# Scores before P times V in the first seven batches, inverse row sums spread by ScalarE, last block scaled by ScalarE and stored by the sync queue

## The chip, the cores and the metric

The kernel runs on one core of a Trainium2 chip, in fp32 (large matmuls as three fp32r products of high and low halves). The metric is the device time of one execution in microseconds (us): 685.59 us before, the median of 3 runs (684.93 to 685.87).

## The reference

One post-norm decoder layer on x of shape (8, 256, 512): softmax attention with 16 heads of 32, a decayed recurrence over a context, and a gated feed-forward net whose weights are cubic splines of control points. Cut to what matters:

```python
def heads(y): return y.reshape(B, T, H, dh).transpose(0, 2, 1, 3)
q, k, v = heads(x @ Wq.T), heads(x @ Wk.T), heads(x @ Wv.T)      # then each times Wdown (32 x 32)
scores = einsum('bhqr,bhkr->bhqk', q_r, k_r) / sqrt(32)
y_r = einsum('bhqk,bhkr->bhqr', softmax(scores), v_r)            # then Wup, then Wo
x = layernorm(x + attention)
r_t = decay * r_(t-1) + ctx_t * ctx_t                            # per feature, a scan over 256 tokens
x = layernorm(x + x * r)
x = layernorm(x + (silu(x @ gate.T) * (x @ up.T)) @ down.T)      # gate, up, down: splines, 2048 wide
```

## The kernel before, in words

It is written without a planner: every engine has its own instruction list, in the order of the code, and waits on semaphores. That order is written out by hand, for each engine in a function of its own: `pe_batch`, `act_batch`, `dve_batch`, `pool_batch`, `sp_batch` for a batch of attention, `..._step` for the feed-forward net. PE stands for TensorE, ACT for ScalarE, DVE for VectorE, POOL for GpSimd, SP for the sync queue.

**Attention.** Eight batches `b`, each in four blocks `m` of four heads; block (b,m) below. For one block, TensorE computes the scores S (L478: 16 matmuls, four 32-row tiles at a time, into PSUM banks 0 to 3). VectorE takes the negated row maxima (`dve_max`, L821, one reduction per bank). ScalarE writes exp(S - max) to `probs` and row sums to `rsum` (`act_exp`, L665, eight activations). TensorE transposes `probs` back into banks 0 to 3 (`pe_t`, L490, 16 transposes; it waits for the exp of each head). ScalarE copies head 0 (`act_heads`, L677, signal `pta`) and VectorE heads 1 to 3 (`dve_heads`, L835, signal `ptv`) to `probsT`. VectorE takes the reciprocal of `rsum` into `rinv` and spreads it over 32 columns a head into `rwide` (`dve_inverse`, L827 and L830). TensorE transposes that (`pe_r`, L498) and ScalarE copies it to `Rb` (L680, signal `ra`). TensorE computes P times V (`pe_pv`, L512, four 32-column tiles at a time, 16 matmuls) once `pta`, `ptv` and `ra` are there. VectorE multiplies with `Rb` into `y` (`dve_y`, L785), ScalarE rounds it to `yT` (`act_yh`, L673) and GpSimd takes the low half (`pool_yl`, L921).

Between S and the transposes TensorE runs projections of this or the next batch: `pe_q`, `pe_k` in m = 0 to 2 (m = 0 has the output projection `pe_o` of the batch before instead), `pe_v0`, `pe_v1` in m = 3. The results leave PSUM by ScalarE (`act_qkh`, L653; `act_v`, L659). `pe_extra` puts in one spline tile (b = 1 to 3, L402, copied by VectorE as `spc`, L773) or one weight job (b from 4, L1096, merged by VectorE as `ws`, L1117) before P times V; `pe_q` of m = 3, and `pe_q(nb, 1)`, run in block m = 1 and 2, reuse its bank and wait for `spc` or `ws`. In block m = 2 the four scans of the recurrence (`dve_scan`, L896) stand on VectorE behind `dve_heads`. `dve_size` (L806) stands in m = 3. GpSimd squares the context (L917), rounds x (L909, L911), applies norms (L957, L1002), multiplies (L965) and adds up splines (L936, L940). Batch 7 (`proj` false) has no projections for a next batch.

**Feed-forward.** Four blocks of 512 tokens, eight groups of hidden units in each (`pe_step`: L303 to L305). After the last block each of its four tiles `t` of 128 tokens is finished by `dve_add` (L1408), `dve_out_stats` (L1412), an aggregation (L1594), variance plus eps and power -0.5 on GpSimd (L1638, L1640), `dve_out` (L1426: subtract mean, times inverse deviation) and a store of 256 KB that GpSimd issues (`pool_out`, L1482); on GpSimd all four stores stand behind the four powers.

## Time and profile before

| | us |
|---|---|
| median of 3 runs | 685.59 |
| the profiled execution's own time | 685.51 |
| its span, first to last instruction | 683.7 |
| 0 to 20, loads and first projections | 20 |
| 20 to 340, attention; TensorE busy 313.8 | 320 |
| 340 to 380, end of attention; TensorE busy 35.0 | 40 |
| 380 to 669, feed-forward; TensorE busy 285.2 | 289 |
| 669 to 683.7, last norm and stores | 14.7 |

The profile is of one execution. A row of a timeline is one instruction, or several alike in a row. The busy time of TensorE is modelled and counts a matmul longer than the distance to the next one, so small waits of TensorE are read from the starts of its instructions.

### The profile page before, as it was taken

How to read it: one execution, taken by the hardware profiler on the slowest of the kernel's cores; microseconds unless marked ns; L12 is line 12 of the kernel's file. 1: busy time of each engine (PE TensorE's matmuls, PEld its weight loads, DVE VectorE, ACT ScalarE, POOL GpSimd, SP SyncE). 2: the span in 40 equal slices, each digit the busy share in tenths (PEclk: the TensorE clock that was granted, in tenths of full speed). 3: DMA queues.
4: the chain of work that ended last, by engine and by line, in shares of the span. 5: the costliest groups of instructions: out<-in, count | busy, mean ns of one | idle time of the engine just before them, and what ended most of it. 6: DMA issues, size and time to landing. Idle time of an engine off the chain costs nothing.

```text
span 683.7 us, 12025 instructions
## 1 busy us (share of the span) xinstructions
PE 656.8 (96%) x4312; PEld 533.8 (78%) x4312; DVE 449.5 (66%) x826; ACT 347.7 (51%) x1002; POOL 294.3 (43%) x351
## 2 busy tenths in 40 slices
PE   9999999999999999999988799999999999999993
PEld 9597887878888788788865577888888888888883
DVE  3567687698686877878778688666544555354434
ACT  5566546637466565656667556552334233333230
POOL 1764486886638767594674836100100001000103
PEclk9999999999999999999999999999999999999997
DMA  9621020030220311121112672741193317340301
GB/s 329 221 80 62 1 87 7 2 125 1 94 62 2 133 52 32 63 72 41 40 65 47 159 173 72 210 105 40 35 239 78 81 32 198 72 101 0 124 1 61
DMA packets 22010, 58.06 MB, mean 85 GB/s; under 512 B 4032, under 2 KB 7232, under 8 KB 21056
## 3 DMA queue, kind: packets, MB, share of 16 engines
q1 hardware_dynamic: 16720, 44.45, 22.5%
q0 software_dynamic: 4944, 12.32, 5.9%
q8 instruction: 35, 0.57, 0.3%
q10 hardware_dynamic: 288, 0.52, 0.2%
q14 instruction: 23, 0.19, 0.1%
HBM read 32.11 MB, written 8.39 MB: 59 GB/s over the span
## 4 chain that ended last, share of the span: by engine, by line
PE 78%; DVE 12%; ACT 6%; issue 2%; POOL 1%; DVEq 0%; POOLq 0%; ACTq 0%
PE bank L303 19%; PE bank L305 18%; PE bank L304 18%; PE bank L490 6%; ACT probs L665 5%; PE bank L478 4%; DVE recurrence_T L896 4%; PE bank L512 4%; DVE minus_max L821 3%; PE bank L1191 2%; PE bank L1096 2%; DVE probsT L835 2%; PE bank L529 1%; PE bank L316 1%; PE bank L498 1%
## 5 line engine op out<-in xcount | busy, mean ns | idle before, releaser
L665 ACT ACTIVATE probs<-bank,minus_max 128x256 f32<-128x256 f32 x256 | 117.3, 486 | 23.8 <-DVE minus_max L821 23.8
L303 PE MATMUL bank<-down,hidden_hi_lo 128*128 128x512 f32 x256 | 100.7, 393 | 1.5 <-DVE hidden_hi_lo L1402 1.5
L305 PE MATMUL bank<-down,hidden_hi_lo 128*128 128x512 f32 x256 | 100.5, 392 | 0.0
L304 PE MATMUL bank<-down,hidden_hi_lo 128*128 128x512 f32 x256 | 100.0, 391 | 0.0
L821 DVE TENSOR_REDUCE minus_max<-bank 128x2 f32<-128x512 f32 x128 | 79.3, 681 | 16.3 <-PE bank L478 16.3
L1398 DVE TENSOR_TENSOR hidden<-bank,silu 128x512 f32<-128x512 f32 x64 | 44.1, 689 | 60.9 <-PE bank L305 58.9
L1356 ACT ACTIVATE silu<-bank 128x512 f32<-128x512 f32 x64 | 38.3, 598 | 82.2 <-PE bank L305 81.3
L1402 DVE TENSOR_TENSOR hidden_hi_lo<-hidden,hidden_hi_lo 128x512 fp32r<-128x512 f32 x64 | 45.5, 711 | 40.9 <-ACT hidden_hi_lo L1369 40.8
L490 PE MATMUL bank<-ident,probs 128*128 128x128 f32 x512 | 65.5, 275 | 6.2 <-ACT probs L665 5.9
L1476 POOL TENSOR_TENSOR ffn_var_eps<-ffn_mean_var,constants 128x4 f32<-128x4 f32 x3 | 0.6, 196 | 156.5 <-DVE ffn_mean_var L1418 156.5
L490 PEld LDWEIGHTS bank<-ident,probs 128*128 128x128 f32 x512 | 56.6, 141 | 14.2 <-ACT probs L665 12.0
L1369 ACT CAST hidden_hi_lo<-hidden 128x512 fp32r<-128x512 f32 x64 | 39.8, 622 | 52.3 <-DVE hidden L1398 52.3
L835 DVE COPY probsT<-bank 128x512 f32<-128x512 f32 x96 | 60.1, 680 | 4.8 <-PE bank L490 4.7
L303 PEld LDWEIGHTS bank<-down,hidden_hi_lo 128*128 128x128 f32 x256 | 48.1, 188 | 11.5 <-DVE hidden_hi_lo L1402 1.9
L305 PEld LDWEIGHTS bank<-down,hidden_hi_lo 128*128 128x128 f32 x256 | 48.0, 188 | 10.3
L665 ACT ACTIVATION_READ_ACCUMULATOR probs<-bank,minus_max 128x1 f32 x256 | 55.9, 219 | 0.0
L304 PEld LDWEIGHTS bank<-down,hidden_hi_lo 128*128 128x128 f32 x256 | 48.1, 188 | 9.7
L303 PE MATMUL bank<-xT_hi_lo,wq_hi 128*128 128x256 f32 x128 | 38.7, 303 | 1.1 <-DVE spline_coef_T_down L773 0.4
L303 PE MATMUL bank<-xT_hi_lo,wk_hi 128*128 128x256 f32 x128 | 38.9, 304 | 0.0
L512 PE MATMUL bank<-probsT,V 128*32 128x256 f32 x512 | 36.8, 385 | 0.4 <-ACT inverse_by_query L680 0.4
L478 PE MATMUL bank<-k_heads,q_heads 32*128 32x256 f32 x512 | 36.7, 400 | 0.0
L305 PE MATMUL bank<-xT_hi_lo,wq_lo 128*128 128x256 f32 x128 | 36.1, 282 | 0.0
(170 smaller groups left out, 1610.8 us busy)
## 6 DMA issues: line engine op xcount, KB each, us to landing
features_by_group<-features_by_cell SPq DMA_DIRECT2D x128, 128.0 KB, 2.4
ctx_squared_T<-in_ctxT SPq DMA_DIRECT2D x8, 512.0 KB, 3.3
xres<-in_x SPq DMA_DIRECT2D x8, 512.0 KB, 4.6
x_in<-x SPq DMA_DIRECT2D x16, 256.0 KB, 3.1
x_residual<-x POOLq DMA_DIRECT2D x4, 1024.0 KB, 8.1
out_x<-x_residual POOLq DMA_DIRECT2D x16, 256.0 KB, 2.8
xin_T<-in_xT SPq DMA_DIRECT2D x7, 512.0 KB, 3.9
x<-x_rows SPq DMA_DIRECT2D x7, 512.0 KB, 4.1
```

Source lines behind the costliest of these rows:

```text
L303: nc.tensor.matmul(out, wh, xh, start=first, stop=False)
L304: nc.tensor.matmul(out, wh, xl, start=False, stop=False)
L305: return nc.tensor.matmul(out, wl, xh, start=False, stop=last)
L478: last = nc.tensor.matmul(S[g][:, t * T:(t + 1) * T], qk[0][at, m, t * P:(t + 1) * P], qk[1][at, m, :], start=True, stop=True)
L490: last = nc.tensor.transpose(S[g][:, kt * T + t * P:kt * T + (t + 1) * P], probs[:, g, t, kt * P:(kt + 1) * P], ident[:])
L512: last = nc.tensor.matmul(MI[g * DH:(g + 1) * DH, 0:T], V[:, kt, h * DH:(h + 1) * DH], probsT[:, g, kt, :], start=kt == 0, stop=kt == TT - 1)
L665: inc(nc.scalar.activation(probs[:, g, t, :], S[g][:, t * T:(t + 1) * T], ACT.Exp, bias=nmax[:, g, t:t + 1], accum_out=rsum[:, t, g:g + 1] ...
L821: inc(nc.vector.tensor_reduce(nmax[:, g, :], S[g][:].rearrange("p (t k) -> p t k", t=TT), AX.X, ALU.max, negate=True), "max")
L835: inc(nc.vector.tensor_copy(probsT[:, g, :, :], S[g][:].rearrange("p (k t) -> p k t", k=2)), "ptv")
L1369: inc(nc.scalar.copy(hid[:, g % 2, 0, j, :], hm[:]), "hh")
L1398: inc(nc.vector.tensor_tensor(hm[:], U[:], sg[:], ALU.mult), "hm")
L1402: inc(nc.vector.tensor_tensor(hid[:, g % 2, 1, j, :], hm[:], hid[:, g % 2, 0, j, :].bitcast(F32), ALU.subtract), "hl")
```

## The change

In batches 0 to 6 the scores of block m+1 are issued ahead of P times V of block m, for m = 0 to 2; from block 3 to the next batch the order stays. In batch 0 the last fold matmul stands between the two. VectorE likewise takes the maxima of block m+1 ahead of `dve_y` of block m, and ScalarE does `act_yh` of block m-1 inside `act_exp` of block m, ahead of the fourth head's exps. The four scans of a batch move from behind `dve_heads(b, 2)` to ahead of `dve_inverse(b, 2)`. In all eight batches the spread copy to `rwide` moves from VectorE to ScalarE, where it is the first thing in `act_heads`. In batch 0 the last low half of Wo is taken inside the maxima of block 1. In the last feed-forward block GpSimd computes one more tiny product a tile (minus mean times inverse deviation), ScalarE applies scale and bias in one activation instead of VectorE's `dve_out`, and the sync queue issues the four stores, each behind its tile.

```diff
 def pe_batch(pe, b):
-        if b == 0:
-            pe_fold_o(pe, 3)
-        pe_pv(pe, b, 0)
-        pe_s(pe, b, 1)
+        if proj:
+            pe_s(pe, b, 1)
+            if b == 0:
+                pe_fold_o(pe, 3)
+            pe_pv(pe, b, 0)
+        else:
+            pe_pv(pe, b, 0)
+            pe_s(pe, b, 1)
...
 def act_exp(act, b, m):
         for g in range(HG):
+            if m and g == HG - 1 and b < B - 1:
+                act_yh(act, b, m - 1)
...
+    def act_wide(act, b, m):
+        act.wait_ge(s["rinv"], 4 * b + m + 1)
+        wait(act, "r", 4 * b + m)
+        src = rinv[:].rearrange("p t (g o) -> p t g o", o=1).to_broadcast([P, TT, HG, DH])
+        inc(nc.scalar.copy(rwide[:].rearrange("p t (g o) -> p t g o", g=HG), src), "rwide")
     def act_heads(act, b, m):
+        act_wide(act, b, m)
...
 def dve_max(dve, b, m):
         for g in range(HG):
+            if b == 0 and m == 1 and g == 2:
+                dve_weight_lo(dve, "o", MT - 1)
...
 def dve_inverse(dve, b, m):
-        wait(dve, "r", 4 * b + m)
+        wait(dve, "rwide", 4 * b + m)
         inc(nc.vector.reciprocal(rinv[:], rsum[:]), "rinv")
-        dve.wait_ge(s["rinv"], 4 * b + m + 1)
-        src = rinv[:].rearrange("p t (g o) -> p t g o", o=1).to_broadcast([P, TT, HG, DH])
-        inc(nc.vector.tensor_copy(rwide[:].rearrange("p t (g o) -> p t g o", g=HG), src), "rwide")
...
+    def dve_max_y(dve, b, m):
+        if b < B - 1:
+            dve_max(dve, b, m + 1)
+            dve_y(dve, b, m)
+        else:
+            dve_y(dve, b, m)
+            dve_max(dve, b, m + 1)
 def dve_batch(dve, b):
+        dve_max_y(dve, b, 1)
         dve_extra(dve, b, 1)
-        if not proj:
-            dve_scan(dve, b, range(2))
+        dve_scan(dve, b, range(KT) if proj else range(2))
         dve_inverse(dve, b, 2)
         dve_heads(dve, b, 2)
-        if proj:
-            dve_scan(dve, b, range(KT))
...
 scalar, after its last step:
+            for t in range(BT):
+                act.wait_ge(s["nm"], t + 1)
+                inc(nc.scalar.activation(res[:, t, :], res[:, t, :], ACT.Identity, bias=fnm[:, t:t + 1], scale=frstd[:, t:t + 1]), "yout")
 vector, last block:
-                if t:
-                    dve_out(dve, NB - 1, t - 1)
-            dve_out(dve, NB - 1, BT - 1)
 gpsimd, last block:
+                inc(nc.gpsimd.tensor_scalar(fnm[:, t:t + 1], fmv[:, t, 0:1], frstd[:, t:t + 1], -1.0, ALU.mult, ALU.mult), "nm")
-            for t in range(BT):
-                pool_out(pool, NB - 1, t)
 sync, at its end:
+            for t in range(BT):
+                sp.wait_ge(s["yout"], BT * (NB - 1) + t + 1)
+                inc(sp.dma_start(out_v[:, BT * (NB - 1) + t, :], res[:, t, :]), "last", 16)
```

## Rows read from the trace of the kernel before

A timeline's columns are: start in us, duration in us, engine, line, operation, out<-in, count, and in brackets the idle time ahead of it with what ended it.

**Rows 1.** Busy time by stretch, attention: PE, PEld, DVE, ACT, POOL, clock, DMA.

```profile
20.00:340.00 320.00, 313.77 (x2639) 255.37 (x2638) 240.38 (x448) 191.04 (x672) 216.49 (x240) 1.00 0.18 59
```

**Rows 2.** Starts of S for block (b,3) and the next batch, b = 1, 3, 4, 5, 6.

```profile
96.78 0.74 PEld L478 LDWEIGHTS bank<-k_heads,q_heads 32*128 32x128 f32 x16 [0.41 <-issue]
108.61 0.74 PEld L478 LDWEIGHTS bank<-k_heads,q_heads 32*128 32x128 f32 x16 [0.41 <-issue]
...
186.85 0.74 PEld L478 LDWEIGHTS bank<-k_heads,q_heads 32*128 32x128 f32 x16 [0.41 <-issue]
197.03 0.74 PEld L478 LDWEIGHTS bank<-k_heads,q_heads 32*128 32x128 f32 x16 [0.41 <-issue]
...
229.24 0.74 PEld L478 LDWEIGHTS bank<-k_heads,q_heads 32*128 32x128 f32 x16 [0.41 <-issue]
240.18 0.74 PEld L478 LDWEIGHTS bank<-k_heads,q_heads 32*128 32x128 f32 x16 [0.41 <-issue]
...
272.40 0.74 PEld L478 LDWEIGHTS bank<-k_heads,q_heads 32*128 32x128 f32 x16 [0.41 <-issue]
283.93 0.74 PEld L478 LDWEIGHTS bank<-k_heads,q_heads 32*128 32x128 f32 x16 [0.41 <-issue]
...
316.14 0.74 PEld L478 LDWEIGHTS bank<-k_heads,q_heads 32*128 32x128 f32 x16 [0.41 <-issue]
326.44 0.74 PEld L478 LDWEIGHTS bank<-k_heads,q_heads 32*128 32x128 f32 x16 [0.41 <-issue]
```

**Rows 3.** Timeline of VectorE, block (1,2), and of its scans in batch 3.

```profile
86.88 2.48 DVE L821 TENSOR_REDUCE minus_max<-bank 128x2 f32<-128x512 f32 x4 [0.60 <-PE bank L478]
89.28 0.68 DVE L773 CAST spline_coef_T_gate<-bank 128x512 fp32r<-128x512 f32 x1
...
94.50 5.73 DVE L896 TENSOR_TENSOR_SCAN recurrence_T<-decay,ctx_squared_T 128x256 f32<-128x256 f32 x4
...
184.56 2.42 DVE L896 TENSOR_TENSOR_SCAN recurrence_T<-decay,ctx_squared_T 128x256 f32<-128x256 f32 x4
```

**Rows 4.** Timeline of GpSimd, block (1,2).

```profile
86.80 0.73 POOL L921 TENSOR_TENSOR yT_lo<-heads_out,yT_hi 128x256 fp32r<-128x256 f32 x1
...
88.17 1.29 POOL L911 TENSOR_TENSOR xT_hi_lo<-xin_T,xT_hi_lo 128x512 fp32r<-128x512 f32 x1
```

**Rows 5.** Weight loads of block (1,2): S, first projection, spline tile.

```profile
85.72 0.74 PEld L478 LDWEIGHTS bank<-k_heads,q_heads 32*128 32x128 f32 x16 [0.41 <-issue]
86.79 0.19 PEld L303 LDWEIGHTS bank<-xT_hi_lo,wq_hi 128*128 128x128 f32 x1 [0.33 <-issue]
...
95.20 0.42 PEld L402 LDWEIGHTS bank<-ident,spline_coef_rows 128*128 128x128 f32 x4 [0.23 <-ACT k_heads L653]
```

**Rows 6.** Weight loads from k to q in blocks (1,2) and (4,2).

```profile
90.08 0.19 PEld L303 LDWEIGHTS bank<-xT_hi_lo,wq_hi 128*128 128x128 f32 x1 [0.36 <-issue]
...
222.39 0.19 PEld L305 LDWEIGHTS bank<-xT_hi_lo,wk_lo 128*128 128x128 f32 x1
222.69 0.19 PEld L303 LDWEIGHTS bank<-xT_hi_lo,wq_hi 128*128 128x128 f32 x1
```

**Rows 7.** One line's instructions: count, duration min/median/max in ns, starts, form.

```profile
L830 DVE COPY row_sum_inverse_wide<-row_sum_inverse x32: 293/295/1425, 26.3 to 363.8; 128x256 f32<-128x256 f32 x32
L673 ACT CAST yT_hi<-heads_out x32: 404/406/408, 33.7 to 367.8; 128x256 fp32r<-128x256 f32 x32
L1369 ACT CAST hidden_hi_lo<-hidden x64: 615/622/625, 379.6 to 666.0; 128x512 fp32r<-128x512 f32 x64
```

**Rows 8.** Timeline of the end, VectorE and GpSimd.

```profile
672.48 0.52 DVE L1426 TENSOR_SCALAR x_residual<-x_residual,ffn_mean_var,ffn_rstd 128x512 f32<-128x512 f32 x1
...
676.34 0.18 DVE L1594 BATCH_NORM_AGGREGATE ffn_mean_var<-ffn_bn_stats 128x2 f32<-128x6 f32 x1
...
677.08 0.54 POOL L1640 TENSOR_TENSOR ffn_rstd<-ffn_var_eps,constants 128x1 f32<-128x1 f32 x1
677.58 2.34 POOL L1482 DMA_DIRECT2D out_x<-x_residual  x4
```

More of the change, by code:

```diff
@@ L212, in program @@
     fst6, fmv = sb("ffn_bn_stats", [P, BT, 6]), sb("ffn_mean_var", [P, BT, 2])
-    fve, frstd = sb("ffn_var_eps", [P, BT]), sb("ffn_rstd", [P, BT])
+    fve, frstd, fnm = (sb(n, [P, BT]) for n in ("ffn_var_eps", "ffn_rstd", "ffn_minus_mean"))
     early, late = ExitStack(), ExitStack()
@@ L279, in program @@
              "fres xt fxh fxl f fh fl w wa ws wh wl wld "
-             "g u silu hm hh hl hused d add bn mv ve rstd yout out moments").split()
+             "g u silu hm hh hl hused d add bn mv ve rstd yout out moments nm last").split()
     s = {n: sem(f"s_{n}") for n in names}
@@ L586, in pe_batch @@
         pe_extra(pe, b, 1)
-        pe_pv(pe, b, 1)
-        pe_s(pe, b, 2)
+        if proj:
+            pe_s(pe, b, 2)
+            pe_pv(pe, b, 1)
+        else:
+            pe_pv(pe, b, 1)
+            pe_s(pe, b, 2)
         if proj:
@@ L603, in pe_batch @@
         pe_extra(pe, b, 2)
-        pe_pv(pe, b, 2)
-        pe_s(pe, b, 3)
+        if proj:
+            pe_s(pe, b, 3)
+            pe_pv(pe, b, 2)
+        else:
+            pe_pv(pe, b, 2)
+            pe_s(pe, b, 3)
         if proj:
@@ L710, in act_batch @@
         act_extra(act, b, 0)
-        act_yh(act, b, 0)
+        if not proj:
+            act_yh(act, b, 0)
         act_exp(act, b, 1)
@@ L720, in act_batch @@
         act_extra(act, b, 1)
-        act_yh(act, b, 1)
+        if not proj:
+            act_yh(act, b, 1)
         act_exp(act, b, 2)
@@ L735, in act_batch @@
         act_extra(act, b, 2)
-        act_yh(act, b, 2)
+        if not proj:
+            act_yh(act, b, 2)
         act_exp(act, b, 3)
@@ L835, in dve_heads @@
             inc(nc.vector.tensor_copy(probsT[:, g, :, :], S[g][:].rearrange("p (k t) -> p k t", k=2)), "ptv")
+    def dve_max_y(dve, b, m):
+        if b < B - 1:
+            dve_max(dve, b, m + 1)
+            dve_y(dve, b, m)
+        else:
+            dve_y(dve, b, m)
+            dve_max(dve, b, m + 1)
     def dve_batch(dve, b):
@@ L849, in dve_batch @@
         if b == 0:
-            for m in range(MT):
+            for m in range(MT - 1):
                 dve_weight_lo(dve, "o", m)
-        dve_y(dve, b, 0)
-        dve_max(dve, b, 1)
+        dve_max_y(dve, b, 0)
         dve_extra(dve, b, 0)
@@ L858, in dve_batch @@
         dve_heads(dve, b, 1)
-        dve_y(dve, b, 1)
-        dve_max(dve, b, 2)
+        dve_max_y(dve, b, 1)
         dve_extra(dve, b, 1)
-        if not proj:
-            dve_scan(dve, b, range(2))
+        dve_scan(dve, b, range(KT) if proj else range(2))
         dve_inverse(dve, b, 2)
         dve_heads(dve, b, 2)
-        if proj:
-            dve_scan(dve, b, range(KT))
-        else:
+        if not proj:
             dve_x2l(dve, 0, 0, B_)
             dve_x2l(dve, 0, 1, C_)
-        dve_y(dve, b, 2)
-        dve_max(dve, b, 3)
+        dve_max_y(dve, b, 2)
         dve_extra(dve, b, 2)
@@ L1420, in dve_out @@
     def dve_out(dve, n, t):
-        if n < NB - 1:
-            dve.wait_ge(s["rstd"], n + 1)
-        else:
-            wait(dve, "rstd", NB + t)
+        dve.wait_ge(s["rstd"], n + 1)
         o = res[:, t, :]
@@ L1640, in _ @@
                 inc(nc.gpsimd.tensor_tensor(frstd[:, t:t + 1], fve[:, t:t + 1], half[:, 2, 0:1], ALU.pow), "rstd")
-            for t in range(BT):
-                pool_out(pool, NB - 1, t)
-            pool.wait_ge(s["out"], 16 * BT * NB)
+                pool.wait_ge(s["rstd"], NB + t)
+                inc(nc.gpsimd.tensor_scalar(fnm[:, t:t + 1], fmv[:, t, 0:1], frstd[:, t:t + 1], -1.0, ALU.mult, ALU.mult), "nm")
+            pool.wait_ge(s["out"], 16 * BT * (NB - 1))
         @block.sync
@@ L1691, in _ @@
                         sp_features(sp, n, g, c)
+            for t in range(BT):
+                sp.wait_ge(s["yout"], BT * (NB - 1) + t + 1)
+                inc(sp.dma_start(out_v[:, BT * (NB - 1) + t, :], res[:, t, :]), "last", 16)
+            sp.wait_ge(s["last"], 16 * BT)
     late.close()
```

## The prediction

> **What bounds it now.** I read the busy time by stretch first. In the 320 us of attention TensorE is busy for 313.8, VectorE for 240, GpSimd for 216 and ScalarE for 191 [rows 1]: TensorE carries this stage, and the reader is to see that only its waits and its own work can shorten it. The table shows the same for the feed-forward net (285 of 289), which the change leaves alone. The busy time hides short waits, so next come the starts of S, block by block. From S of (b,3) to S of the next batch TensorE has nearly the same work each time, yet it takes 11.83 us in batch 1, 10.18 in batch 3, 10.94 in 4, 11.53 in 5 and 10.30 in 6 [rows 2]. The timeline of VectorE tells why: its four scans behind the copies of block (1,2) last 5.73 us and end at 100.2, so the maxima of (1,3), whose S was issued at 96.78, start 2.5 us late (in (1,2) they came 1.16 behind S, here they can't before 100.4), the exps too, and the transposes wait; in batch 3 the scans last 2.42 and end before they can hurt [rows 2, 3]. Last I looked at the weight loads inside a block: from k to q of (1,2) there are 0.36 us without a load, of (4,2) 0.30 between two loads that else come every 0.12 [rows 6]. There q waits for a bank that VectorE empties behind its maxima (the copy of 0.68 starts at 89.28, the load of q at 90.08) [rows 3, 6].
>
> **The change, part by part.** Times with a dash, such as S', are those of the changed kernel; 0 is the start of S' of the block in question.
>
> *Scores first, maxima first.* The number of matmuls stays. S starts about 1.04 us earlier against the rest (P times V from its start to the next S is about a microsecond: from the spline tile at 95.20, 0.6 us of it, to S at 96.78) [rows 2, 5], and maxima, exps and the bank of q come as much earlier against the transposes. In m = 1 and 2 of batches 1 to 6 the wait of q goes. Its bank is ready at 3.57 (four maxima from 1.16 on, 0.6 apart) + 0.35 (`dve_y`, now behind them) + 0.6 = 4.6, and q comes at 1.04 + 4.0 = 5.0 instead of 4.0. A wait is worth 0.36 + 0.07 (loads of 0.19 overlap by that) = 0.43 in batches 1 to 3 and 0.30 - 0.12 = 0.18 in 4 to 6 [rows 3, 6]: 6 x 0.43 + 6 x 0.18 = 3.7 us. The cover is thin, 0.4 us.
>
> *Late maxima of (b,3).* With the scans ahead of the inverse, VectorE is free when S' of (b,3) ends. Against the undisturbed 10.18 of batch 3, batch 1 has 1.65 to gain and batch 2, with the same scans, as much; for batches 4 to 6, whose weight job is shorter than four transposes, I take 10.0 as undisturbed (an estimate: batch 6's 10.30 less a short wait): 0.95, 1.55, 0.30. Batch 0 has scans like batch 4's, 0.9 [rows 2]. Sum 7.0 us.
>
> *The scans' new place.* This is the price. Inverse, spread, transpose L498 and the copy to `probsT` of (b,2) now stand behind the scans, and on ScalarE, which waits for the inverse at the head of `act_heads`, so do `pta`, `Rb` and the copies of k and q for the next batch. Scans start at 3.57 + 0.35 + 0.6 = 4.5 in batches 1 to 3. Alone they take 2.4; beside GpSimd 5.73, more than twice that [rows 3]. In (1,2) GpSimd's work began with `pool_yl` at 86.80, 1.08 behind S [rows 4, 5]; now it waits for `act_yh`, which stands behind six exps, until about 5.0. So the first scan runs alone (0.6) and the other three each let one GpSimd operation pass, of 0.73, 0.6 and 1.29 [rows 4], plus 0.35 of their own: 1.05 + 0.95 + 1.65. The inverse starts at 4.5 + 4.25 = 8.8. Behind it: 0.25 the inverse, 0.35 the spread on ScalarE (a cast of the same size takes 0.41 [rows 7], less what overlaps), 0.6 the copy of head 0, 0.3 `Rb`, 0.4 the copy of k, for which the spline tile waits [rows 5]: 8.8 + 1.9 = 10.7. Undisturbed that tile starts at 95.20 - 85.72 - 0.43 + 1.04 = 10.05 [rows 5]. Loss 0.65 to 0.7 in each of batches 1 to 3, 2.1 us together. `ptv` is there at 8.8 + 0.2 + 1.9 = 10.9, S' of (b,3) at 11.3, so that is no second wait. In batches 0 and 4 to 6 GpSimd has little to do right behind `pool_yl` (there it waits for a weight job), the inverse starts at 7.4 to 8.1, under the 8.15 from which it costs: 0. From both sides: scans alone, no loss at all; all as slow as 5.73, 1.5 to 2.1 a batch.
>
> The Trainium skill (SBUF — State Buffer, "Who interferes with whom") says that a VectorE instruction with two SBUF inputs contends with a GpSimd instruction that reads SBUF, for a shared port pair that one holds for its whole instruction; the 5.73 against 2.42 of the same four scans agree [rows 3]. By that rule the scans' new place is as exposed as the old one wherever GpSimd has work, which speaks against the move.
>
> *Spread on ScalarE.* Taken from VectorE are 32 copies of 0.29 (up to 1.43 when GpSimd is beside) [rows 7]. In batches 0 to 6 this lies beside TensorE's projections: 0. On ScalarE 0.35 and a wait for the inverse come ahead of `pta`; `pta` there has over 1 us until S', except in m = 2 (above). In blocks (7,2) and (7,3), where TensorE has no projections and P times V waits for VectorE's three copies, they come 0.3 earlier each: 0.6 us. If ScalarE's queue decides instead, up to 0.4 each is lost.
>
> *Turning the array over.* Each of the 21 moved pairs had the changes column tiles to row tiles (0.41 without a load) and row tiles to the full array (0.33) [rows 2, 5]. New are full array to S, S to P times V, P times V to the full array, which attention before shows hardly or not at all. The idle times seen are the last matmul's run plus about 0.1, so I take 0; bounds: 0.4 less (for none of the turn-overs is free today) to 0.25 more a pair, and of these I keep -1 to +4 us for the 21.
>
> *Batch 0, low half of Wo.* q of (0,1) waits for all four low halves before and after. The last of them now stands behind three others and two maxima, which ends as S did before: 0, give or take 0.3.
>
> *The end.* Two of VectorE's scalings stood ahead of the last aggregation at 676.34, about 0.44 each of their 0.52 [rows 8]: it comes at 675.5. Then, by the distances before, variance 0.26, power 0.26, its end and the new product 0.9, at 676.9 ScalarE's scaling of 128x512, 0.62 as its casts [rows 7], 677.55. The sync queue issues the last store at 677.6. Before, GpSimd issued four in 2.34 from 677.58, the last at 679.34 [rows 8]. 1.7 us, and 0.1 as the last store has the queues to itself: 1.8. Bounds 1.0 (a slow start of this queue) to 2.6.
>
> The Trainium skill (DMA: Bandwidth & Descriptors, its opening table) gives about 1 us to the first byte for a DMA issued from GpSimd and 0.6 from sync; as an estimate from that page the end would gain 2.2. No row here shows the two side by side for a store.
>
> **Sum.** 3.7 + 7.0 + 0.6 + 1.8 - 2.1 = 11.0. The profiled execution took 685.5, as the median (685.6) did: 674.5 us.
>
> **Rivals.** (a) *ScalarE's queue in (b,2).* The inverse comes at 10.2 rather than 8.8 in batches 1 to 3 (the scans meet one GpSimd operation each, as before) and at 9 in 4 to 6: 2.1 x 3 + 0.8 x 3 = 8.7 lost instead of 2.1, 681.1. For it: 5.73 and 11.53 in batch 5; against: GpSimd starts 4 us later in the block. Between this and the forecast anything is possible. (b) *Turn-over.* 0.2 more for each of the 21: 4.2, 678.7. (c) *No loss.* Scans alone everywhere: 672.4. (d) *Nothing from the order.* S' needs all four copies of `probsT`, P times V needed them one after the other; if S' waits for them as long as the transposes waited, only the ends remain: 683.1. Against: in undisturbed blocks the copies end over 1 us before P times V. (e) *Slower.* The place is block (b,2) of all seven batches: the inverse behind four scans. The gains without it are 13.1, so it decides from 13.1 / 7 = 1.9 us a batch, an inverse at 10.05. Were the scans 6.5 us in every batch, it would be 11.0 and the loss 2.85 x 7 = 20: 692.4. The longest row is 5.73 [rows 3], and by it batches 0 and 4 to 6 would lose 1.6 to 1.9 and the others 2.1, some 13.3 in all, which is no change.
>
> **How the numbers follow.** Forecast 0.58, (a) 0.13, (b) 0.09, (c) 0.09, (d) 0.05, (e) 0.04, anything else 0.02. The range 671.5 to 681.5 takes in (a), (b), (c) and the bounds of the end and of batch 0. About 0.2% (1.4 us) is what a measurement of this kernel can tell from no change. Faster 0.93, same 0.03, slower 0.04.
>
> **What the new profile would show.** S' of (b,3) to S of the next batch close to 10.2 in batches 1 to 3 and 10.0 in 4 to 6, with no wait of the transposes for exps. No gap between k and q. The scans of batches 1 to 3 at about 4.3 us, the inverse near 8.8 behind S', S' to S' of block (b,2) some 0.7 above the 10.65 of block (b,1). The first loads of S', of P times V and of q with 0.2 to 0.4 of idle time. The last store issued by sync near 6 us before the end. The prediction is wrong if scans and GpSimd meet oftener than this, if the unseen turn-overs cost more, or if the removed waits of q come back as waits for ScalarE.

## The result and the profile after

| | before | after |
|---|---|---|
| median, us | 685.26 | 669.90 |
| profiled execution's own time | 685.51 | 670.12 |
| its span | 683.7 | 668.3 |

The medians here are of four executions each. The ratio of the times is 0.9776, interval 0.9764 to 0.9789. The change gains 15.4 us where 11.0 were forecast, and 669.9 lies below the range. The two spans differ by the same 15.4, so the traces can be laid side by side. The time is gained here (starts before and after; the difference is the gain up to that point):

| point | before | after | gained so far |
|---|---|---|---|
| S of (0,0) | 20.29 | 20.38 | -0.1 |
| S of (7,0) | 326.44 | 315.99 | 10.45 |
| S of (7,3) | 357.04 | 346.19 | 10.85 |
| first silu of the feed-forward net | 378.15 | 367.78 | 10.4 |
| 17th silu | 459.42 | 449.50 | 9.9 |
| last (64th) silu | 664.55 | 652.72 | 11.8 |
| first add of the last block | 669.41 | 657.55 | 11.9 |
| end of the span | 683.7 | 668.3 | 15.4 |

Attention gave what its terms said, less a loss that didn't come; 1.9 us come from a stage that the change doesn't touch; and the end gave 3.5 instead of 1.8.

Attention first. Busy time by stretch, in the order of [rows 1], of attention up to S of (7,0):

```profile
20.00:316.00 296.00, 294.07 (x2527) 243.31 (x2526) 206.31 (x397) 190.51 (x671) 208.80 (x229) 1.00 0.19 62
```

TensorE is busy for 294 of 296 us (99.3%, where [rows 1] had 98.1%). Starts of S in the changed kernel, from the timeline of weight loads: (1,2), (1,3), (2,0); then (3,3), (4,0) and (5,3), (6,0).

```profile
83.47 0.74 PEld L478 LDWEIGHTS bank<-k_heads,q_heads 32*128 32x128 f32 x16 [0.17 <-issue]
...
94.12 0.74 PEld L478 LDWEIGHTS bank<-k_heads,q_heads 32*128 32x128 f32 x16 [0.17 <-issue]
...
105.33 0.74 PEld L478 LDWEIGHTS bank<-k_heads,q_heads 32*128 32x128 f32 x16 [0.41 <-issue]
...
179.25 0.74 PEld L478 LDWEIGHTS bank<-k_heads,q_heads 32*128 32x128 f32 x16 [0.17 <-issue]
190.45 0.74 PEld L478 LDWEIGHTS bank<-k_heads,q_heads 32*128 32x128 f32 x16 [0.41 <-issue]
...
263.13 0.74 PEld L478 LDWEIGHTS bank<-k_heads,q_heads 32*128 32x128 f32 x16
274.14 0.74 PEld L478 LDWEIGHTS bank<-k_heads,q_heads 32*128 32x128 f32 x16 [0.41 <-issue]
```

Against [rows 2]: (1,3) takes 11.21, (3,3) 11.20, (5,3) 11.01. In the kernel before the same blocks took 11.83, 10.18 and 11.53. All are now alike, 1.0 above the undisturbed 10.2 because P times V of (b,2) has moved into them, and none is left with a wait that the others don't have. Block (1,2) takes 10.65, as long as (1,1), where the forecast had it 0.7 longer. The whole batch fell from 44.97 to 42.56 us. The gap between k and q, 0.36 us without a load in [rows 6], is closed; the last load of k and the first of q in (1,2):

```profile
88.28 0.19 PEld L305 LDWEIGHTS bank<-xT_hi_lo,wk_lo 128*128 128x128 f32 x1
88.40 0.19 PEld L303 LDWEIGHTS bank<-xT_hi_lo,wq_hi 128*128 128x128 f32 x1
```

In (1,2) VectorE (first four rows; the third is from a narrower window and holds the second and third scan alone) and GpSimd (last four), from their timelines:

```profile
84.63 2.48 DVE L847 TENSOR_REDUCE minus_max<-bank 128x2 f32<-128x512 f32 x4 [2.37 <-PE bank L478]
...
87.96 3.30 DVE L921 TENSOR_TENSOR_SCAN recurrence_T<-decay,ctx_squared_T 128x256 f32<-128x256 f32 x4
...
88.56 1.75 DVE L921 TENSOR_TENSOR_SCAN recurrence_T<-decay,ctx_squared_T 128x256 f32<-128x256 f32 x2
...
91.18 0.17 DVE L853 RECIPROCAL row_sum_inverse<-row_sum 128x8 f32<-128x8 f32 x1
...
88.58 1.18 POOL L946 TENSOR_TENSOR yT_lo<-heads_out,yT_hi 128x256 fp32r<-128x256 f32 x1 [1.63 <-ACT yT_hi L687]
89.71 1.00 POOL L934 CAST xT_hi_lo<-xin_T 128x512 fp32r<-128x512 f32 x1
90.79 1.54 POOL L936 TENSOR_TENSOR xT_hi_lo<-xin_T,xT_hi_lo 128x512 fp32r<-128x512 f32 x1
92.28 0.61 POOL L934 CAST xT_hi_lo<-xin_T 128x512 fp32r<-128x512 f32 x1
```

The scans take 3.30, not 4.25. The second began at 88.56, a hair ahead of `pool_yl` (88.58), and ran its 0.67 undisturbed; the third then waited for `pool_yl`, the fourth for the cast of 1.00; the subtraction, 1.29 in [rows 4], came when they were nearly through. The inverse starts at 91.18, 7.7 behind S' and not 8.8.

The end, from the timelines of VectorE, GpSimd, ScalarE and the sync queue: last aggregation, last product, last scaling, and the four stores with the time from the first to the last:

```profile
663.56 0.18 DVE L1619 BATCH_NORM_AGGREGATE ffn_mean_var<-ffn_bn_stats 128x2 f32<-128x6 f32 x1
...
664.75 0.27 POOL L1664 TENSOR_SCALAR ffn_minus_mean<-ffn_mean_var,ffn_rstd 128x1 f32<-128x1 f32 x1
...
665.05 0.81 ACT L1586 ACTIVATE x_residual<-x_residual,ffn_minus_mean,ffn_rstd 128x512 f32<-128x512 f32 x1 [0.71 <-POOL ffn_minus_mean L1664]
...
661.34 4.88 SPq L1716 DMA_DIRECT2D out_x<-x_residual  x4
```

The stores by line (duration of the issue min/median/max in ns, first and last start) with the time from issue to landing, after, then before (where the line has all sixteen stores of the output):

```profile
L1716 SPq DMA_DIRECT2D out_x<-x_residual x4: 332/338/344, 661.3 to 665.9; - x4
...
DMA to landing us min/median/max: 2.0/2.0/2.0
```

```profile
L1482 POOL DMA_DIRECT2D out_x<-x_residual x16: 539/542/743, 494.4 to 679.4; - x16
...
DMA to landing us min/median/max: 2.4/2.8/3.1
```

From the last aggregation to the last issue: 2.3 us (663.56 to 665.9), before 3.0 (676.34 [rows 8] to 679.4). From the last issue to the end of the span: 2.4 (to 668.3), before 4.3 (to 683.7). The second difference is the larger one, and the forecast gave it 0.1. It has two parts: before, the last store took 3.1 us to land and the span went on for 1.2 more, after, 2.0 and 0.4.

### The profile page after: what moved, and what is told of

It is laid out like the page before. It is cut to its first block, busy times and chain, and to the rows that moved or that the text cites. A ratio compares the mean times of both kernels' runs of the same rounds, so it can differ in the third digit from the quotient of the medians.

```text
span 668.3 us, 12061 instructions
## 1 busy us (share of the span) xinstructions
PE 648.3 (97%) x4312; PEld 532.6 (80%) x4312; DVE 421.9 (63%) x790; ACT 360.5 (54%) x1038; POOL 291.5 (44%) x351
## 4 chain that ended last, share of the span: by engine, by line
PE 90%; DVE 4%; ACT 4%; issue 1%; POOL 0%; DVEq 0%; POOLq 0%; ACTq 0%
PE bank L303 22%; PE bank L305 21%; PE bank L304 21%; PE bank L490 8%; PE bank L478 5%; PE bank L512 5%; PE bank L1216 2%; PE bank L1121 2%; ACT probs L679 2%; PE bank L498 1%; PE bank L529 1%; PE bank L402 1%; PE bank L316 1%; PE bank L1190 1%; ACT hidden_hi_lo L1394 1%
## 5 line engine op out<-in xcount | busy, mean ns | idle before, releaser
L490 PE MATMUL bank<-ident,probs 128*128 128x128 f32 x512 | 62.5, 273 | 3.1 <-ACT probs L679 3.1
L305 PEld LDWEIGHTS bank<-down,hidden_hi_lo 128*128 128x128 f32 x256 | 48.0, 188 | 10.2
L946 POOL TENSOR_TENSOR yT_lo<-heads_out,yT_hi 128x256 fp32r<-128x256 f32 x24 | 20.0, 832 | 52.7 <-ACT yT_hi L687 52.7
```

What stands on the lines that cost most here:

```text
L305: return nc.tensor.matmul(out, wl, xh, start=False, stop=last)
L490: last = nc.tensor.transpose(S[g][:, kt * T + t * P:kt * T + (t + 1) * P], probs[:, g, t, kt * P:(kt + 1) * P], ident[:])
```

## Experiments

Ratios are to the kernel before on the same chip, with 95% intervals. "The late stretch" is the time from the 17th to the 64th silu of the feed-forward net, almost nothing but matmuls of 512 columns: 205.13 us before (459.42 to 664.55), 203.22 after (449.50 to 652.72).

**The two halves of the change: tail_only and no_tail.** The first is the kernel before with the edits of the last block alone, the second the changed kernel without them.

```diff
+    fve, frstd, fnm = (sb(n, [P, BT]) for n in ("ffn_var_eps", "ffn_rstd", "ffn_minus_mean"))
+            for t in range(BT):
+                act.wait_ge(s["nm"], t + 1)
+                inc(nc.scalar.activation(res[:, t, :], res[:, t, :], ACT.Identity, bias=fnm[:, t:t + 1], scale=frstd[:, t:t + 1]), "yout")
...
+                inc(sp.dma_start(out_v[:, BT * (NB - 1) + t, :], res[:, t, :]), "last", 16)
```

> The kernel before with the edits of the last block alone (product on GpSimd, scaling on ScalarE, stores by the sync queue). In the changed kernel the way from the first add of the last block to the end of the span is 10.75 us instead of 14.3, so 3.5 us of the 15.4 should be here: 681.8 us. Theory A: TensorE's distance between the 512-column matmuls of the feed-forward net (0.229 us before, 0.2267 in the changed kernel) has to do with attention's order; it stays 0.229 here. Rival: it has to do with the changed lists of ScalarE, GpSimd and sync at the end; then it is 0.2267 here and the time is 680 us.

> The changed kernel with the last block as before (only attention is changed). 669.9 + 3.5 = 673.4 us if the parts add up. Theory A: the distance of the matmuls in the feed-forward net stays at 0.2267 us. Rival: it goes back to 0.229, and the time is 675 us.

Measured: tail_only 679.36 us, 0.9914 (0.9898 to 0.9931); no_tail 675.07, 0.9853 (0.9838 to 0.9868). The rival was right both times. The edits of the last block are worth 5.7 us on the kernel before and 5.2 on the attention edits (675.07 to 669.90), of which their own place, the last 14 us, holds only 3.5. The late stretch tells the rest: 203.21 in tail_only (459.14 to 662.35), 205.19 in no_tail. Something in these edits makes the matmuls ahead of them faster: on average 0.2271 us apart instead of 0.2294.

**The tile behind it: pad32 and fnm_last.** The edits add one tile of 16 bytes a partition, `ffn_minus_mean`, ahead of most others. In the compiled program all later tiles stand 32 bytes further: `features_by_group` starts at byte 82048 instead of 82016. pad32 is the kernel before with an unused tile of that size there; fnm_last is the changed kernel with its tile allotted last, so that no other moves.

```diff
 pad32
     fve, frstd = sb("ffn_var_eps", [P, BT]), sb("ffn_rstd", [P, BT])
+    sb("unused", [P, BT])
 fnm_last
-    fve, frstd, fnm = (sb(n, [P, BT]) for n in ("ffn_var_eps", "ffn_rstd", "ffn_minus_mean"))
+    fve, frstd = sb("ffn_var_eps", [P, BT]), sb("ffn_rstd", [P, BT])
...
     res = sb("x2_residual", [P, BT, D], F32, late)
+    fnm = sb("ffn_minus_mean", [P, BT], F32, late)
```

> The kernel before with one more tile of 16 bytes a partition, ffn_minus_mean's place, that nothing uses. The edits of the last block alone brought 5.7 us where 3.5 lie behind the last matmul, and the feed-forward matmuls went from 0.229 us apart to 0.2267. Theory B: the new tile moves every later tile by 32 bytes, from an address of 32 modulo 64 to one of 0 modulo 64 (features, low halves of weights, down weights), and TensorE reads these faster: 0.2267 us apart here and 683.0 us. Rival: the other edits (two semaphores, longer lists of ScalarE, GpSimd, sync) do it: 0.229 and 685.0 us.

> The changed kernel with ffn_minus_mean allocated behind all other tiles, so that no tile moves against the kernel before. Theory B: the distance of the feed-forward matmuls goes back to 0.229 us and 2 us are lost: 671.9 us. Rival: nothing changes, 669.9 us.

Measured: pad32 683.26, 0.9971 (0.9959 to 0.9982); fnm_last 671.8, 0.9803 (0.9789 to 0.9816). The 17th and the last silu, ScalarE's timeline, of before, pad32 and fnm_last:

```profile
459.42 0.60 ACT L1356 ACTIVATE silu<-bank 128x512 f32<-128x512 f32 x1 [1.48 <-PE bank L305]
...
664.55 0.60 ACT L1356 ACTIVATE silu<-bank 128x512 f32<-128x512 f32 x1 [2.08 <-PE bank L305]
```

```profile
458.95 0.60 ACT L1357 ACTIVATE silu<-bank 128x512 f32<-128x512 f32 x1 [1.45 <-PE bank L306]
...
662.14 0.60 ACT L1357 ACTIVATE silu<-bank 128x512 f32<-128x512 f32 x1 [2.05 <-PE bank L306]
```

```profile
449.01 0.60 ACT L1382 ACTIVATE silu<-bank 128x512 f32<-128x512 f32 x1 [1.47 <-PE bank L306]
...
654.14 0.60 ACT L1382 ACTIVATE silu<-bank 128x512 f32<-128x512 f32 x1 [2.08 <-PE bank L306]
```

205.13, 203.19 and 205.13 us: an unused tile alone brings the gain, and the whole change without the shift doesn't have it. That much is shown: 1.9 of the 15.4 us are an accident of the memory layout.

**Which tiles: pad_feat, pad_lo, pad_w.** Unused bytes at two or three places, so that only some tiles get another place mod 64 bytes: the later ones (features and all behind), the earlier ones (`hidden`, the low halves, `features_by_cell`, `moments`), the low halves alone.

```diff
 pad_feat
+    sb("unused_attention", [P, BT], F32, attn)
+    sb("unused_late", [P, BT], F32, late)
     feat = sb("features_by_group", [P, NG, 2, BLK], F32R, late)
 pad_lo, in addition
+    sb("unused_early", [P, BT], F32, late)
     hm = sb("hidden", [P, BLK], F32, late)
 pad_w
+    sb("unused_early", [P, BT], F32, late)
     w_lo = [sb(f"weights_lo_{n}", [P, NG, GROUP], F32R, late) for n in ("gate", "up")]
+    sb("unused_late", [P, BT], F32, late)
     by_cell = sb("features_by_cell", [P, CELLS, 2, BLK], F32R, late)
```

> The kernel before with 32 unused bytes allotted only ahead of features_by_group: the tiles hidden, weights_lo, by_cell and moments keep their start at 32 mod 64 bytes, features_by_group, hidden_hi_lo and the down-projection tiles that follow go to 0 mod 64. Theory that these later tiles (the moving operand among them) set the matmuls' distance: about 683.3 us, distance of 512-column matmuls in the feed-forward stage 0.2267 us as in pad32. Rival, the low halves of the weights set it: about 685.0 us, distance 0.229.

> The kernel before with unused bytes that move hidden, weights_lo, by_cell and moments to 0 mod 64 bytes and leave features_by_group and all later tiles at 32 mod 64 (the complement of pad_feat; attention's tiles stay at their alignment too). Theory that the low halves' place counts in the hidden matrices' matmuls (278 recorded distances fell from 0.231 to 0.227 in pad32, 588 of the output matrix's from 0.2285 to 0.227): the 0.4 us that pad_feat gained and this one's gain add up to pad32's 2.0, so about 684.0 us. Rival, both operands must be moved before either helps: 685.3 us and unchanged distances in the hidden matrices.

> The kernel before with weights_lo alone moved to 0 mod 64 bytes, every other tile of the feed-forward stage at 32 mod 64. Theory that the weight load of the low halves is what is late: the distances in the hidden matrices fall as in pad_lo, the same 684.0 us. Rival, the moving operands' place counts as well: smaller gain than pad_lo, 684.6 to 685.3 us.

Measured: pad_feat 684.7, 0.9994 (0.9985 to 1.0003), late stretch 204.78, so nearer the rival; pad_lo 686.24, 1.0016 (1.0007 to 1.0025), 206.30; pad_w 686.25, 1.0018 (1.001 to 1.0027), 206.38. The last two are slower than before, which neither theory had. But in both the tiles behind the second pad stand 64 bytes further than before, and I had taken for granted that this changes nothing.

**All tiles together by 64, 96 and 128 bytes.**

```diff
     fve, frstd = sb("ffn_var_eps", [P, BT]), sb("ffn_rstd", [P, BT])
+    sb("unused", [P, 16])    # pad96: [P, 24], pad128: [P, 32]
```

> The kernel before with 64 unused bytes where pad32 has 16 (taking 32): every later tile moves by 64 bytes and so keeps its place mod 64, but not mod 128. Theory that the places mod 128 or beyond count, which pad_lo and pad_w changed by 64 for all tiles behind the second pad: distance of 512-column matmuls 0.231 us as in these two, about 686.3 us. Rival, only the place mod 64 counts and pad_lo and pad_w were slow for their mixture: as before, 685.3 us and 0.229.

> The same with 96 unused bytes: later tiles at 0 mod 64, as in pad32, and 64 bytes further than there. Rule mod 64: 683.3 us and distance 0.2267. Rule by finer place: between 683 and 686 with another distance than 0.2267.

> The same with 128 unused bytes: places mod 128 are those of the kernel before. Rule mod 64 or mod 128: 685.3 us and distance 0.229. If places over more than 128 bytes count, another time.

| all later tiles moved by | ratio to before | late stretch |
|---|---|---|
| 0 (before) | 1 | 205.13 |
| 32 (pad32) | 0.9971 | 203.19 |
| 64 (pad64) | 1.0016 (1.0007 to 1.0025) | 206.22 |
| 96 (pad96) | 0.9977 (0.9968 to 0.9986) | 203.81 |
| 128 (pad128) | 1.0004 (0.9995 to 1.0013) | 205.40 |

Moved by 32 or 96, that is to starts at 0 mod 64, the stage is fast; at 32 mod 64 it is slow. Within each kind a shift by 64 bytes more changes it by another 0.6 to 1.1 us. pad_lo and pad_w fit this: both are as slow as pad64, so with the later tiles in that place nothing is won by moving the low halves or the other early tiles. And pad_feat gains little: some of the hidden matrices' matmuls get slower, 0.2338 us from the second one of `spline_coef_T_gate` to the one of `weights_lo_gate`, 0.2297 before, 0.2275 in pad32. No run that moved only some of the tiles has more than 0.35 us of the gain. Whether each operand's own place counts or the places of two against each other (`spline_coef_T_gate` itself moves in none of these runs), and by what mechanism, is open.

**The stores: sp_store.** Before, with the last four stores on the sync queue; VectorE still scales, no tile moves.

```diff
-            for t in range(BT):
-                pool_out(pool, NB - 1, t)
...
+            for t in range(BT):
+                sp.wait_ge(s["yout"], BT * (NB - 1) + t + 1)
+                inc(sp.dma_start(out_v[:, BT * (NB - 1) + t, :], res[:, t, :]), "last", 16)
```

> The kernel before with the last four stores issued by the sync queue alone; scaling stays on VectorE, no tile moves. Theory that the stores' landing and GpSimd's closing count beside the issue: last issue 678.25 instead of 679.38 (1.1) and issue to span end 2.4 instead of 4.36 (2.0), 3.0 gained: about 682.0 us. Rival, only the issue counts: 683.9.

Measured 682.75, 0.9958 (0.9945 to 0.997), a gain of 2.9 against the 3.0 of the theory and the 1.8 of the rival. The last scaling, timeline of VectorE, and the stores by line (span 680.1):

```profile
677.14 0.55 DVE L1426 TENSOR_SCALAR x_residual<-x_residual,ffn_mean_var,ffn_rstd 128x512 f32<-128x512 f32 x1 [0.71 <-POOL ffn_rstd L1640]
```

```profile
L1692 SPq DMA_DIRECT2D out_x<-x_residual x4: 333/338/344, 672.5 to 677.7; - x4
...
DMA to landing us min/median/max: 2.0/2.0/2.0
```

The last issue comes when the scaling ends, and 2.4 us later the span ends, as in the changed kernel. From the first add of the last block (668.89) to the end of the span are 11.2 us, where the kernel before has 14.3 and the changed one 10.8. So of the 3.5 us at the end 3.1 are the queue's, 1.2 ahead of the last issue and 1.9 behind it, and 0.5 come from scaling on ScalarE with the shorter chain on VectorE.

**The scans' place: scans_old.** The changed kernel with the scans behind the copies of (b,2), as before.

```diff
+        if not proj:
+            dve_scan(dve, b, range(2))
-        dve_scan(dve, b, range(KT) if proj else range(2))
         dve_inverse(dve, b, 2)
         dve_heads(dve, b, 2)
+        if proj:
+            dve_scan(dve, b, range(KT))
```

> The changed kernel with the four scans of batches 0 to 6 back behind the copies of block (b,2). Theory: the scans' place makes the late maxima of (b,3), so most of the 7 us come back: S of (b,3) to S of the next batch grows from 11.2 to about 13 in batches 1 and 2, 12.1 to 12.6 in 4 and 5; 677 us. Rival: since S and the maxima come 1 us earlier against the transposes, the place of the scans hardly matters any more: 670 to 672 us.

Measured 678.45, 0.990 (0.9885 to 0.9915), 8.5 us above the changed kernel. VectorE's scans and the S of (1,3) and (2,0):

```profile
94.57 5.54 DVE L924 TENSOR_TENSOR_SCAN recurrence_T<-decay,ctx_squared_T 128x256 f32<-128x256 f32 x4
100.03 2.45 DVE L847 TENSOR_REDUCE minus_max<-bank 128x2 f32<-128x512 f32 x4
...
95.86 0.74 PEld L478 LDWEIGHTS bank<-k_heads,q_heads 32*128 32x128 f32 x16 [0.17 <-issue]
...
108.47 0.53 PEld L478 LDWEIGHTS bank<-k_heads,q_heads 32*128 32x128 f32 x12 [0.41 <-issue]
```

5.54 us again, the maxima 4.2 behind S, block (1,3) 12.61 instead of 11.21. Over the seven batches the blocks (b,3) lose 8.5 us, which is the whole difference; the other blocks are unchanged. The late maxima come from the scans' place.

**What the scans cost in their new place: yh_g1, pv_first, scans_six.** yh_g1 lets GpSimd begin half a microsecond earlier, by placing `act_yh` ahead of the second head's exps.

```diff
-            if m and g == HG - 1 and b < B - 1:
+            if m and g == 1 and b < B - 1:
```

> The changed kernel with ScalarE's first normalised copy placed ahead of the second head's exponentials, so that GpSimd's subtraction starts about 0.5 us earlier in the block of the scans. Theory that the scans' price is the number of GpSimd operations that they meet: three instead of two, scans 4.25 us in all, inverse sums ready 8.65 behind the block's start, some 0.65 us a batch lost in batches 1 to 3: about 671.9 us. Rival, the slack of 0.6 takes it: 669.9 to 670.3.

Measured 671.26, 0.9793 (0.978 to 0.9807). VectorE, GpSimd and S of (1,2) and (1,3):

```profile
87.83 4.33 DVE L921 TENSOR_TENSOR_SCAN recurrence_T<-decay,ctx_squared_T 128x256 f32<-128x256 f32 x4
92.08 0.17 DVE L853 RECIPROCAL row_sum_inverse<-row_sum 128x8 f32<-128x8 f32 x1
...
87.83 1.22 POOL L946 TENSOR_TENSOR yT_lo<-heads_out,yT_hi 128x256 fp32r<-128x256 f32 x1 [1.64 <-ACT yT_hi L687]
88.99 1.01 POOL L934 CAST xT_hi_lo<-xin_T 128x512 fp32r<-128x512 f32 x1
90.08 1.53 POOL L936 TENSOR_TENSOR xT_hi_lo<-xin_T,xT_hi_lo 128x512 fp32r<-128x512 f32 x1
...
83.33 0.74 PEld L478 LDWEIGHTS bank<-k_heads,q_heads 32*128 32x128 f32 x16 [0.17 <-issue]
...
94.51 0.74 PEld L478 LDWEIGHTS bank<-k_heads,q_heads 32*128 32x128 f32 x16 [0.17 <-issue]
```

Now three operations are met, the 1.53 among them: scans 4.33 where the forecast of the change had 4.25, inverse 8.75 behind S where it had 8.8, block (1,2) 11.18, which is 0.5 more than 10.65. Three batches make 1.5, and the median is 1.4 higher. So the forecast's working was right for three meetings; the changed kernel has two, by half a microsecond of ScalarE's queue. The Trainium skill (SBUF — State Buffer, "Who interferes with whom") has one engine hold the shared port pair for a whole instruction; that a scan waits out one GpSimd instruction each time, and takes 1.03 to 1.69 us instead of 0.67, agrees.

pv_first is the changed kernel with the old order of P times V, maxima and `act_yh`, so that GpSimd begins early and the scans still stand ahead of the inverse:

```diff
-        if proj:
-            pe_s(pe, b, 1)
...
-            pe_pv(pe, b, 0)
...
+        pe_pv(pe, b, 0)
+        pe_s(pe, b, 1)
```

(and likewise for the other blocks, the maxima and `act_yh`).

> The changed kernel with P times V ahead of the next scores again, the maxima behind dve_y and act_yh ahead of the exps; the scans stay ahead of the inverse, the spread stays on ScalarE. Theory: two things come back. TensorE waits between k and q in (b,1) and (b,2) of batches 1 to 6 (3.7 us); and since GpSimd starts on act_yh's result at once, the four scans meet it each time (5 us instead of 3.4) and the inverse comes later against an L498 that comes 1 us earlier: about 2 us a batch in batches 1 to 3 and 0.5 to 1 in 4 to 6. In all 10 to 14 us, 680 to 684 us. Rival: the scans' place alone carries the gain, and only the waits of q come back: 673.6 us.

Measured 682.82, 0.9964 (0.995 to 0.9977), within what was expected, though the batches share it otherwise: (3,2) takes 14.10, and in batches 4 to 6 the scans run alone in 2.43 and (b,2) loses nothing (10.66). In (1,2) the scans take 5.55 and the inverse comes 9.6 behind S:

```profile
86.04 0.74 PEld L478 LDWEIGHTS bank<-k_heads,q_heads 32*128 32x128 f32 x16 [0.41 <-issue]
...
90.20 5.55 DVE L898 TENSOR_TENSOR_SCAN recurrence_T<-decay,ctx_squared_T 128x256 f32<-128x256 f32 x4
95.68 0.17 DVE L834 RECIPROCAL row_sum_inverse<-row_sum 128x8 f32<-128x8 f32 x1
```

The block takes 13.07 us, where it took 11.06 before the change. With the old order the move of the scans costs 2 us in that block, which is more than (1,3) wins from it (10.20 without the P times V, 11.83 before); the two edits need each other. The times say the same. tail_only has the attention of before and the tiles and the end of the changed kernel, 679.4 us. With the new order alone (scans_old) it is 678.5, about 1 us less; with the scans' move alone (pv_first) 682.8, 3.5 more; with both 669.9, 9.5 less. The spread is on ScalarE in all three.

scans_six puts two more scans (repeats, whose results the next ones overwrite) ahead of the four in each of batches 0 to 6:

```diff
+        if b < B - 1:
+            for k in range(2):
+                inc(nc.vector.tensor_tensor_scan(rsT[:, k, :], dec[:, k:k + 1].to_broadcast([P, T]),
+                                                 cin[:, k, :], 0.0, ALU.mult, ALU.add), "twice")
+            dve.wait_ge(s["twice"], 2 * b + 2)
```

> The changed kernel with two more scans (of the same data, written twice) ahead of the four in batches 0 to 6. In the changed kernel the spread row sums are ready 0.6 us before TensorE asks for them in block (b,2). Theory: that is all the cover there is; two scans of 0.6 to 1.3 us each (they meet GpSimd) use it up and what is over stops TensorE: 1.0 to 2.0 us a batch, 7 to 14 us in all, 677 to 684 us, with the stop ahead of the transpose of the row sums in (b,2). Rival: VectorE has slack in that block that takes them: under 3 us in all, 670 to 673 us.

Measured 685.17, 0.9999 (0.9988 to 1.0009), above the 677 to 684 that were expected. In batches 1 to 3 the inverse comes 10.3 behind S and the block takes 12.70. So the slower outcome that the prediction priced as rival (e) is real and lies near: two more scans eat the whole gain. In (6,2) the block takes 14.80 instead of 10.50, from these rows of VectorE and GpSimd:

```profile
310.27 6.37 DVE L926 TENSOR_TENSOR_SCAN recurrence_T<-decay,ctx_squared_T 128x256 f32<-128x256 f32 x4
...
312.31 3.74 DVE L926 TENSOR_TENSOR_SCAN recurrence_T<-decay,ctx_squared_T 128x256 f32<-128x256 f32 x1
...
311.79 0.63 POOL L1177 DMA_DIRECT2D makers_hidden<-in_makers  x1
312.41 0.56 POOL L1178 DMA_DIRECT2D masks_hidden<-in_masks  x1
312.97 2.52 POOL L995 TENSOR_TENSOR residual_odd<-residual_odd,recurrence_plus_one 128x512 f32<-128x512 f32 x2
```

The second row is from a narrower window. This one scan of the four took 3.74 us: it began at 312.31, as GpSimd issued its DMAs, and ended only when both operations of the 2.52 were over.

**The spread: wide_dve.** The changed kernel with the spread copy on VectorE, as before.

```diff
 def act_heads(act, b, m):
-        act_wide(act, b, m)
...
 def dve_inverse(dve, b, m):
-        wait(dve, "rwide", 4 * b + m)
+        wait(dve, "r", 4 * b + m)
         inc(nc.vector.reciprocal(rinv[:], rsum[:]), "rinv")
+        dve.wait_ge(s["rinv"], 4 * b + m + 1)
+        src = rinv[:].rearrange("p t (g o) -> p t g o", o=1).to_broadcast([P, TT, HG, DH])
+        inc(nc.vector.tensor_copy(rwide[:].rearrange("p t (g o) -> p t g o", g=HG), src), "rwide")
```

> The changed kernel with the spread of the inverse row sums on VectorE again. Theory: TensorE hides it in batches 0 to 6, also in (b,2), where the spread by VectorE (0.3 us) is as far ahead of L498 as ScalarE's, unless it meets GpSimd (up to 1.4 us, which costs 0.5 a batch in three batches); (7,2) and (7,3) lose 0.3 us each: 670.3 to 672 us. Rival: its move was needed for the new order: 674 us or more.

Measured 674.35, 0.9839 (0.9824 to 0.9854): 4.4 us above the changed kernel, the rival's side. Blocks (b,2) of batches 1 to 3 take 0.3 more each, (7,2) again 9.05 instead of 8.67; and in (6,2) this (VectorE, then GpSimd) costs 2.4 there and 1.1 in (6,3):

```profile
303.41 3.14 DVE L855 COPY row_sum_inverse_wide<-row_sum_inverse 128x256 f32<-128x256 f32 x1
...
303.31 0.56 POOL L1175 DMA_DIRECT2D masks_hidden<-in_masks  x1
303.87 2.52 POOL L992 TENSOR_TENSOR residual_odd<-residual_odd,recurrence_plus_one 128x512 f32<-128x512 f32 x2
```

A copy of 0.29 us took 3.14. So 3.4 of the 4.4 us hang on this one meeting in batch 6.

**A step further: all_eight.** The order of the change in the eighth batch too, for the maxima and `act_yh` as well.

```diff
-        if proj:
-            pe_s(pe, b, 1)
...
-        else:
-            pe_pv(pe, b, 0)
-            pe_s(pe, b, 1)
+        pe_s(pe, b, 1)
+        pe_pv(pe, b, 0)
```

> The changed kernel with the new order (scores and maxima ahead of P times V) in the eighth batch too. Theory that the waits of q behind k are gone there as in the other batches: 0.95 in each of (7,2) and (7,3) and a little in (7,1): about 668.0 us. Rival, ScalarE's copies and exponentials at the stage's end take it back: 669.9.

Measured 668.97, 0.9758 (0.9745 to 0.9771); span 667.2 against 668.3. The interval overlaps that of the change, so a gain of about 1 us rests on the two spans and medians only. Half of what the theory said came. S of (7,2) to S of (7,3) takes 8.06 instead of 8.67, from the timeline of weight loads:

```profile
336.31 0.74 PEld L478 LDWEIGHTS bank<-k_heads,q_heads 32*128 32x128 f32 x16
...
344.37 0.77 PEld L478 LDWEIGHTS bank<-k_heads,q_heads 32*128 32x128 f32 x16 [0.91 <-issue]
```

The 0.91 without a load ahead of S shows that S waits there; P times V used to stand in that gap.

## Why the prediction was wrong, step by step

- *Waits of q, 3.7 us.* Right. Blocks (b,1) and (b,2) fell from 11.06 to 10.65 in batches 1 to 3 and from 10.67 to 10.50 in 4 to 6: 3.5. With the old order (pv_first) block (1,1) takes 11.07 again and (4,1) 10.67. (The sum for the bank of q, 3.57 + 0.35 + 0.6, is 4.5 and not 4.6.)
- *Late maxima of (b,3), 7.0.* Right. The batches together gave 10.55; less 3.5 this leaves 7.05, and scans_old shows the place. For a single batch the term is good to half a microsecond at best: block (5,3) took 11.53 in the kernel before and 10.95 in sp_store, which has the same attention. That the length of (b,3) would be "close to 10.2" left out the P times V that moves into it.
- *The scans' new place, 2.1 lost.* This step failed, by the number of meetings: the block lost nothing, where 2.1 us were forecast. Its times were right: scans from 4.49 behind S' (forecast 4.5), `pool_yl` at 5.1 (about 5.0), a scan that meets `pool_yl` or the cast 1.0 to 1.2. But it let the first scan alone run undisturbed, so that three met something. The second one starts 0.6 behind the first, at 5.09, and `pool_yl` at 5.11: the two came within 0.02 us, and VectorE was first, in all three batches. That leaves two meetings, 3.30 us, an inverse at 7.7, and the block has its slack of half a microsecond left. yh_g1 gives the forecast's case with the forecast's numbers. At a tie both counts should have had a price: case (c), no loss, had 0.09, and with it the upper bound of the end gives 671.6, the low end of the range.
- *Turning the array over, 0.* Right. From the last matmul ahead of a turn-over to the first behind it are 0.20 to 0.31 us in the new places, the same as in the old ones.
- *Spread on ScalarE, 0.6.* In (7,2) 0.37 came (9.04 to 8.67). Half a microsecond was given back by the first silu (10.85 to 10.4); but the stretch from S of (7,3) to it, 21.59 us here and 21.11 before, took 21.20 in yh_g1 and 21.82 in no_tail with the same code of batch 7, so what the spread has to do with it isn't shown. And the value of this edit isn't 0.6: without it the changed kernel is 4.4 slower (wide_dve), 3.4 of them by one meeting in batch 6. The forecast saw it as a copy beside projections and missed that behind the scans it is on the same thin path, and in (6,2) beside GpSimd's DMAs.
- *The end, 1.8.* Mis-sized: 3.5. The issue comes 0.9 + 0.7 = 1.6 earlier against the first add (shorter VectorE chain, then no queue of stores), nearly the forecast, though ScalarE's scaling takes 0.81 and not 0.62. The other 1.9 us lie behind the issue: stores from GpSimd took 2.4 to 3.1 to land and the span ended 4.3 after the last one; from the sync queue all take 2.0 and the span ends after 2.4. sp_store shows it alone. The sign "near 6 us before the end" for the last issue fits only the end of the kernel before (677.6 to 683.7); from the sum it was 4.3, and 2.4 came. The Trainium skill (DMA: Bandwidth & Descriptors, its opening table) has the sync queue 0.4 faster to the first byte; the estimate of 2.2 for the end, worked out from it, points the right way and is still short by 1.3.
- *Not in the sum: the place of the tiles, 1.9.* The prediction said that the change leaves the feed-forward net alone. It does in its instructions, not in its addresses.
- *Not in the sum: 0.5 lost between the first and the 17th silu.* These take 81.72 after and 81.27 before; without the tiles' shift 81.91 (fnm_last) and 81.88 (no_tail), and with it and the old attention 81.12 (tail_only), so the loss comes with the attention edits and not with the end. But wide_dve (81.08) and scans_six (81.11) have most of these edits and not the loss. It lies in two steps, from the 9th to the 11th silu (6.25 and 4.80 instead of 5.95 and 4.51), where the last norm of batch 7 on VectorE stands ahead of the product of `hidden`, which comes 1.39 behind its silu instead of 1.04. Why it comes later is open.

The gap of 4.4 us in order of time: up to S of (7,0) 10.45 instead of 8.6, 1.85 more; from there to the first silu -0.1 instead of 0.6, 0.7 less; to the 17th silu 0.5 less; the tiles' place 1.9 more; the end 1.7 more. Together 4.3.

## What to carry to other kernels

Two engines that slow each other down are priced by counting which instructions meet, each start beside each start; a shift of half a microsecond decides one meeting, so give the forecast both counts and let the range hold both. Two edits can bring little or a loss alone and most of the gain together, as the order and the scans' place did here, so try them alone and together. Where a transfer is the last thing, look up what lies behind its issue as well, by queue. And when an edit adds a tile, see which other tiles it moves: here a shift of 32 bytes was worth 1.9 of the 15.4 us, and a kernel that is compared by fractions of a per cent should be compared at the same addresses.

## What the runs showed of the hardware

- The distance of 512-column fp32r matmuls depended on where tiles start: on average 0.2271 to 0.2277 us where all tiles behind the unused one start at 0 mod 64 bytes (pad32, pad96), 0.2294 to 0.2307 where they start at 32 mod 64 (before, pad64, pad128); over a stretch of 205 us that is 1.3 to 3.0 us. Moving only some of them brought 0.35 us (pad_feat) or nothing (pad_lo, pad_w), and a further 64 bytes for all changes it by 0.6 to 1.1 us.
- A scan of 0.67 us that met one GpSimd instruction took 1.03 to 1.69. A VectorE instruction that met GpSimd while it issued DMAs waited through the next two GpSimd operations: a copy of 0.29 took 3.14, a scan 3.74 (wide_dve and scans_six, once each).
- A store of 256 KB from the sync queue landed in 2.0 us each time, from GpSimd in 2.4 to 3.1. From the last issue to the end of the span it was 2.4 us and 4.3.
- ScalarE's scaling with scale and bias from memory, 128x512, took 0.81, its cast of the same size 0.62.
